# Attention decoder on one core: fp32 products for C, the inner norm's weight moved into a matrix, two norms moved to GpSimd, and a new hand-written order

## The chip, the cores and the metric

One core of a Trainium2 chip runs the whole program. The metric is the device time of one execution in microseconds (us), the median of three runs. The engines are called by their names in the trace: PE (TensorE, with PEld for its weight loads), DVE (VectorE), ACT (ScalarE), POOL (GpSimd), and SP (SyncE, which here only issues DMAs).

## The reference, cut to what matters

The input x is 128 sequences of 64 tokens by 128 features, ctx is as large. Everything is fp32.

```
def attn(x):                       # linear attention, 16 heads of 64, 32 features
    q, k, v = x @ Wq + bq, x @ Wk + bk, x @ Wv + bv
    qp, kp  = exp(q @ wq_feat), exp(k @ wk_feat)
    D_inv   = 1 / (qp . sum_n kp + 1e-6)
    context = einsum(kp, v)        # one 32 x 64 matrix a head
    return (qp @ context * D_inv) @ Wproj + bproj
def xattn(x, ctx):                 # softmax attention, 16 heads of 8
    return softmax(Q K^T / sqrt(8)) V @ Wo + bo
def ffn(x):
    h = gelu(x @ tern(W_fc).T)     # 128 -> 512, weights -1, 0 or 1
    h = (h - mean(h)) * rsqrt(var(h) + eps) * ln_w + ln_b
    return h @ tern(W_proj).T      # 512 -> 128
x = layernorm(x + attn(x)); x = layernorm(x + xattn(x, ctx)); x = layernorm(x + ffn(x))
```

## The kernel before, in words

The 128 sequences are 16 batches of 8. In every tile the 128 partitions hold features or tokens and the 512 columns are the 8 times 64 tokens. A batch goes through three blocks.

The first block: `k0` to `k3` and `q0` to `q3` are projections with exp behind them (three fp16 products each, of the two fp16 parts of x and of the weights). `ks`, `kst`, `dT` and `bc` make and spread the denominators. `g0` to `g7` (L329) form G = x^T kp, one sequence each, on 64 of the 128 rows of the array: the even ones on the upper half, the odd ones on the lower. An fp32 matmul shows as two instructions in the trace. `c0` to `c7` (L341) multiply each G by Mh, the product of Wv and Wproj of each head, which gives C; `o` multiplies qT by C. The 16 heads of a C take a column tile of 32 each, so that four run at once. Here G is kept as two fp16 parts, Gh (ACT, L581) and Gl (DVE, L822), and M as Mh and Ml: three fp16 products a head, 48 matmuls a C.

The second block: `x1s` (ACT L601, POOL L1081) splits x1 into fp16 parts, a transposing DMA turns it, `qproj`, `kproj`, `vproj` project, `qpack`, `kpack` and `rows` are DMAs that lay out rows for `score` and `prob`, `score` is followed by eight maxima on DVE (L880), `prob` by exp on ACT, `pv`, `oturn`, `cs` and `proj` end it.

The third block: `up0` to `up3` with GELU (ACT L675), `stat` (DVE, POOL), `gs` (POOL L1114), a multiplication of the 128x512 GELU output by ln_w, `gh` (ACT L688) and `gl` (POOL L1119), the fp16 parts, a transposing DMA, and `down0` to `down3`, eight fp16 products each (L507, L508), with `tpj`, the ternary weights.

The norms behind the blocks are `ap1` (ACT L595, with a shift that POOL works out in L1072 and L1076), `ap2` (ACT) and `ap3` (DVE L858); their inverse roots come from POOL (L1058, L1061). For the last two batches the transposes are done by PE, with other weights.

Order: three strings (HEAD, PERIOD, TAIL) list the steps. `g3@1` is step g3 of the batch one behind the period's own, a + puts the step's copy on ACT, not on DVE. PERIOD is run for n = 1 to 14. All engines go through one list, each does its own steps in that order and never passes a waiting one. The eight PSUM banks are dealt out in turn in the same order: a step's first matmul waits until the bank's last user, eight uses back, has been read.

Of the kernel before, what the change touches and what calls it, by code (L numbers as in the profile page):

```python
# [39 lines left out]
prob0@2 prob1@2 st1@1 st3@5 down0@4 ap1+@1 csplit@1 down1@4 ab2@3 ks pv0@2 kst g0+ x1s@1 g1+ g2+ g3 ab1@1 pv1@2 xb down2@4 split@-1 kproj@1 loadx@-1  # L40
q0 down3@4 q1 up0@3 c0 gs0@3 c1 up1@3 up2@3 stat@3 up3@3 qproj@1 oturn0@2 q2 loadc kpack@1 q3 c2+ oturn1@2 gs1@3 g4 g5 g6 g7 cs0@2 c3+ dT qpack@1
k0@-1 gl0@3 gh0@3 k1@-1 c4+ c5+ score0@1 k2@-1 cs1@2 proj0@2 score1@1 k3@-1 gh1@3 gs2@3 vproj@1 gl1@3 proj1@2 c6+ gs3@3 c7+ gh2@3 rows@1 gh3@3 st2@2
bc gl2@3 gl3@3 ap3@5 o ap2+@2
# [4 lines left out]
vproj@2 c0+@1 c1+@1 g4+@1 q0@1 q1@1 c2+@1 ap3@6 c3+@1 gl1@4 q2@1 st3@5 gh1@4 ap2+@3 gs3@4 kst@1 gl2@4 score0@2 q3@1 score1@2 gh2@4 g5@1 g6+@1 gl3@4
dT@1 kpack@1 c4@1 g7+@1 c5@1 gh3@4 kproj@1 down0@4 vproj@1 tw@1 c6+@1 c7@1 down1@4 bc@1 rows@2 ab1@2 up0@3 down2@4 ab2@3 up1@3 up2@3 down3@4 gs0@3
stat@3 up3@3 o@1 prob0@2 st1@1 gl0@3 ap3@5 gs1@3 gl1@3 prob1@2 qpack@1 st3@4 gs2@3 gh0@3 pv0@2 oturn0@2 pv1@2 oturn1@2 gs3@3 ap1+@1 flip+@1 proj0@2  # L50
gh1@3 qproj@1 proj1@2 ap2+@2 st2@2 down0@3 ap3@4 down1@3 ab2@2 flip3@2 gh2@3 gh3@3 score0@1 score1@1 up0@2 gl2@3 up1@2 up2@2 gl3@3 up3@2 rows@1
# [27 lines left out]
def decoder_kernel(nc, a, out):  # L79
# [3 lines left out]
    GS = 2.0 ** -4  # L83
    two = range(2)

    with ExitStack() as ctx:
# [451 lines left out]
        def act_program(e):  # L538
# [151 lines left out]
            for name, s, t, on_act in PLAN:  # L690
# [22 lines left out]
                elif name in ("k", "q", "g", "prob", "up", "gh"):  # L713
                    {"k": kexp, "q": qexp, "g": gmat, "prob": prob, "up": up, "gh": ghi}[name](s, t)
# [4 lines left out]
                elif on_act:  # L719
                    {"c": cmat, "turn": turn}[name](s, t)  # L720

        def dve_program(e):
# [16 lines left out]
            def mh(c2):  # L739
                for c in range(2 * c2, 2 * c2 + 2):  # L740
                    hi, lo_ = [v[:, :].rearrange("p (c k a n) -> p c k a n", c=2, k=4, a=2)[:, c // 2, :, c % 2, :] for v in (Mh, Ml)]
                    w.wait_ge(s_mhh, c + 1)
                    e.scalar_tensor_tensor(lo_, bank[uses["mh", 0, c][0]][:, :].rearrange("p (k n) -> p k n", k=4), 1 / GS, hi,
                                           ALU.mult, ALU.subtract).then_inc(emptied("mh", 0, c)[0], 1)

# [623 lines left out]
```

## Time and profile before

| | |
|---|---|
| median of 3 runs | 671.31 us (670.25 to 672.45) |
| profiled execution, its own time | 668.43 us |
| span of its instructions | 666.6 us |
| mean granted TensorE clock | 0.975 |
| PE, DVE, ACT, POOL busy | 589.2, 548.2, 489.1, 457.0 us |

The span runs from the first to the last instruction. An engine's busy time is the time in which at least one of its instructions was open, so that PE's holds also the latency behind the last matmul of a row. The times below are starts from the beginning of the span.

### The profile page before, as it was taken

To read this page: it belongs to the slowest core of one execution; us is meant where nothing else is said; L and a number is where in the kernel's file an instruction comes from. 1 tells how busy PE (TensorE), PEld (TensorE's weight loads), DVE (VectorE), ACT (ScalarE), POOL (GpSimd) and SP (SyncE) were. 2 spreads that over 40 slices of the span, in tenths; PEclk is the share of its full clock that TensorE was granted. 3 is DMA by queue.
4 is the path that set the end of the run, shared out by engine and by line. 5 is a ranking of instruction groups with operands and counts; after the bars stand their busy time and mean duration, and the time that the engine had idled before them with its cause. 6 is when DMAs were issued, how large, how long until landed. Compare 5 with 4: busy or idle time off the path is not lost.

```text
span 666.6 us, 35171 instructions
## 1 busy us (share of the span) xinstructions
PE 589.2 (88%) x15392; PEld 417.9 (63%) x15392; DVE 548.2 (82%) x1365; ACT 489.1 (73%) x922; POOL 457.0 (69%) x563
## 2 busy tenths in 40 slices
PE   8997898989899889989998899989899899897675
PEld 5774656576666657566666657566576657565363
DVE  1864677888878978998999898998899989888786
ACT  3655485969688786968798687968788787777543
POOL 3152143877777786886978778876888777976632
PEclk8998999999999999999999899999999999799689
DMA  8005040435534346534573347334354446352501
GB/s 331 33 2 137 5 136 16 120 76 120 82 76 131 83 137 93 126 76 122 92 117 103 84 137 94 119 81 131 84 93 128 83 137 100 97 97 48 131 3 47
DMA packets 116170, 65.14 MB, mean 98 GB/s; under 512 B 94321, under 2 KB 100850, under 8 KB 115890
## 3 DMA queue, kind: packets, MB, share of 16 engines
q1 hardware_dynamic: 116018, 62.91, 40.7%
q8 instruction: 121, 1.98, 1.2%
q14 instruction: 31, 0.25, 0.2%
HBM read 17.27 MB, written 4.19 MB: 32 GB/s over the span
## 4 chain that ended last, share of the span: by engine, by line
PE 31%; DVE 25%; DMA 10%; ACT 9%; SPq 8%; POOL 8%; issue 8%; POOLq 0%; DVEq 0%; ACTq 0%
SPq L1214 7%; DMA pack<-Ql 6%; DVE mx L880 5%; DVE st L845 5%; DVE yo L858 3%; DVE Ql L864 3%; PE bank L329 3%; PE bank L361 3%; PE bank L453 3%; DVE qT L818 2%; ACT L675 2%; DMA gT<-gs 2%; PE bank L341 2%; POOL rstd L1061 2%; PE bank L297 2%
## 5 line engine op out<-in xcount | busy, mean ns | idle before, releaser
L822 DVE SCALAR_TENSOR_TENSOR Gl<-bank,Gh 128x512 f16<-128x512 f32 x128 | 81.2, 684 | 18.9 <-ACT Gh L581 18.4
L341 PE MATMUL bank<-Mh,Gh 128*32 128x128 f16 x2048 | 94.8, 223 | 1.4 <-DVE Gl L822 0.7
L880 DVE TENSOR_REDUCE mx<-bank 128x8 f32<-128x512 f32 x128 | 79.1, 682 | 20.4 <-PE bank L418 20.4
L341 PE MATMUL bank<-Ml,Gh 128*32 128x128 f16 x2048 | 94.3, 221 | 1.1 <-issue 1.0
L341 PE MATMUL bank<-Mh,Gl 128*32 128x128 f16 x2048 | 94.3, 221 | 0.8 <-issue 0.6
L651 ACT ACTIVATE PT<-bank 128x512 f32<-128x512 f32 x128 | 65.0, 615 | 21.5 <-PE bank L439 21.4
L341 PEld LDWEIGHTS bank<-Mh,Gh 128*32 128x32 f16 x2048 | 55.6, 97 | 35.8 <-issue 19.8
L566 ACT ACTIVATE kp<-bank 128x512 f32<-128x512 f32 x64 | 39.8, 622 | 50.1 <-PE bank L280 49.9
L581 ACT ACTIVATE Gh<-bank 128x512 f16<-128x512 f32 x128 | 69.2, 619 | 8.8 <-PE bank L329 6.4
L1114 POOL TENSOR_TENSOR gall<-gall,lnr 128x512 f32<-128x512 f32 x56 | 71.7, 1280 | 3.9 <-DVE st L845 3.9
L1119 POOL TENSOR_TENSOR gs<-gall,gs 128x512 f16<-128x512 f32 x56 | 64.8, 1163 | 11.3 <-ACT gs L688 9.9
L329 PE MATMUL bank<-kp,xs 64*128 64x512 f32 x256 | 70.4, 620 | 0.0
L1061 POOL TENSOR_TENSOR rstd<-ve,mhalf 128x4 f32<-128x4 f32 x64 | 65.4, 1022 | 5.3
L595 ACT ACTIVATE x<-x,nmr,rstd 128x128 f32<-128x128 f32 x128 | 52.8, 494 | 17.4 <-POOL nmr L1076 17.2
L361 PE MATMUL bank<-Cb,qT 128*64 128x128 f32 x1024 | 59.4, 274 | 2.4 <-DVE qT L818 2.3
L545 ACT ACTIVATE Cb<-bank 128x512 f32<-128x512 f32 x95 | 55.6, 624 | 5.2 <-PE bank L341 4.4
L361 PEld LDWEIGHTS bank<-Cb,qT 128*64 128x64 f32 x1024 | 55.6, 137 | 5.2 <-DVE qT L818 4.8
L341 PEld LDWEIGHTS bank<-Ml,Gh 128*32 128x32 f16 x2048 | 56.5, 98 | 2.0 <-issue 2.0
L341 PEld LDWEIGHTS bank<-Mh,Gl 128*32 128x32 f16 x2048 | 56.1, 98 | 1.5 <-issue 1.5
L688 ACT ACTIVATE gs<-gall 128x512 f16<-128x512 f32 x56 | 36.0, 644 | 26.3 <-DMA gT<-gs 26.3
L573 ACT ACTIVATE qT<-bank,qb 128x512 f32<-128x512 f32 x64 | 42.4, 694 | 5.3 <-PE bank L288 4.9
L818 DVE TENSOR_TENSOR qT<-qT,bank 128x512 f32<-128x512 f32 x64 | 39.7, 682 | 7.8 <-PE bank L320 7.2
(194 smaller groups left out, 1661.3 us busy)
## 6 DMA issues: line engine op xcount, KB each, us to landing
pack<-Qh SPq DMA_DIRECT2D x64, 128.0 KB, 2.6
xT<-in_xT SPq DMA_DIRECT2D x16, 256.0 KB, 3.1
xs<-in_x_nat SPq DMA_DIRECT2D x16, 256.0 KB, 3.7
cxT<-in_cxT SPq DMA_DIRECT2D x16, 256.0 KB, 4.1
Kp<-Kh SPq DMA_DIRECT2D x32, 128.0 KB, 3.2
pack<-Ql SPq DMA_DIRECT2D x32, 128.0 KB, 2.7
out_y<-yo SPq DMA_DIRECT2D x15, 256.0 KB, 2.4
Kp<-Kl SPq DMA_DIRECT2D x16, 128.0 KB, 3.1
```

Of the source, the lines that this page charges most:

```text
L329: e.matmul(bk[:, :], xs[s % 2][r0:r0 + 64, tile(t)], kp[r0:r0 + 64, tile(t, 512)], start=True, stop=True).then_inc(done, 1)
L341: m = e.matmul(bk[32 * j:32 * j + 32, tile(g_)], G[b % 4][:, tile(hh, 32)], M[:, tile(hh)], start=(G is Gh and M is Mh), stop=(M is Ml))
L361: m = e.matmul(bk[64 * bb:64 * bb + 64, 0:128], qT[:, tile(8 * g_ + b, 64)], Cb[b][:, tile(g_)], start=False, stop=(g_ == 3))
L545: e.activation(dst, src, ACT.Copy, scale=scale).then_inc(emptied(name, s, t)[0], 1)
L581: e.activation(Gh[b % 4][:, :], bank[uses["g", s, b][0]][:, :], ACT.Copy, scale=GS).then_inc(s_gth, 1)
L651: e.activation(PT[tp][:, tile(j, 512)], bank[uses["prob", s, i][0]][:, :], ACT.Exp, scale=SM).then_inc(emptied("prob", s, i)[0], 1)
L818: e.tensor_tensor(v, v, bank[uses["bc", s, t][0]][:, :].rearrange(by_head, g=4), ALU.mult).then_inc(emptied("bc", s, t)[0], 1)
L822: e.scalar_tensor_tensor(Gl[b % 4][:, :], bank[uses["g", s, b][0]][:, :], GS, Gh[b % 4][:, :], ALU.mult, ALU.subtract).then_inc(emptied("g ...
L880: e.tensor_reduce(to, bank[uses["score", s, i][0]][:, :].rearrange("p (g b k) -> p g b k", g=2, b=4), AX.X, ALU.max).then_inc(emptied("sco ...
L1061: e.tensor_tensor(rstd[k][:, :], ve[k][:, :], mhalf[:, :], ALU.pow).then_inc(s_rstd[k], 1)
L1114: e.tensor_tensor(g[t][:, :], g[t][:, :], lnr[:, :], ALU.mult).then_inc(s_gs, 1)
L1119: e.tensor_tensor(gs[t % 2][:, 512:1024], g[t][:, :], gs[t % 2][:, 0:512], ALU.subtract).then_inc(s_gl, 1)
```

## The change

- C: G and M stay fp32 in one tile each (GT, Mh). A C is 16 fp32 matmuls instead of 48 fp16 ones; its stationary operand is 32 columns of GT, its moving operand 128 columns of Mh. Each G is copied once, by ACT or by DVE (four of the eight in PERIOD by each), instead of by ACT and then DVE.
- The inner norm's weight: ln_w is multiplied into the down projection's weights once, at the start, and the product is kept in two fp16 parts, tph and tpl. `down` has 12 products instead of 8; `gs` and the load of lnr go.
- `ap1` and `ap3` are done by POOL, as four tensor_scalar of 128x128 each; POOL's two small steps for ap1's shift go. `ap2` stays on ACT.
- HEAD, PERIOD and TAIL are new.

```
-wk wb small1 k0 WkT k1 k2 loadx zeros k3 mh0 mh1 g0+ g1+ split split@1 Wvp g2+ g3+ ...
+zeros mh0 mh1 wk wq k0 Wvp k1 WqT k2 q0 small1 wb nbeta WkT loadx g0+ g1+ g2+ Wff g3+ ...
...
-                for g_ in range(4):
-                    for G, M in ((Gh, Mh), (Gl, Mh), (Gh, Ml)):
-                        for j in range(4):
-                            hh = 4 * g_ + j
-                            m = e.matmul(bk[32 * j:32 * j + 32, tile(g_)], G[b % 4][:, tile(hh, 32)], M[:, tile(hh)], ...
+                for hh in range(H):
+                    g_, j = hh // 4, hh % 4
+                    m = e.matmul(bk[32 * j:32 * j + 32, tile(g_)], GT[b % 4][:, tile(hh, 32)], Mh[:, tile(hh)], start=True, stop=True)
...
                     for c in range(4):
-                        e.matmul(bk[:, 0:128], gT[t][:, tile(c)], tpj[:, tile(c)], start=(c == 0), stop=False)
-                        m = e.matmul(bk[:, 0:128], gT[t][:, tile(4 + c)], tpj[:, tile(c)], start=False, stop=(c == 3))
+                        e.matmul(bk[:, 0:128], gT[t][:, tile(c)], tph[:, tile(c)], start=(c == 0), stop=False)
+                        e.matmul(bk[:, 0:128], gT[t][:, tile(c)], tpl[:, tile(c)], start=False, stop=False)
+                        m = e.matmul(bk[:, 0:128], gT[t][:, tile(4 + c)], tph[:, tile(c)], start=False, stop=(c == 3))
...
-                w.wait_ge(*filled("g", s, b))
-                e.activation(Gh[b % 4][:, :], bank[uses["g", s, b][0]][:, :], ACT.Copy, scale=GS).then_inc(s_gth, 1)
+                copy("g", s, b, GT[b % 4][:, :])
...
-                w.wait_ge(s_gth, 8 * s + b + 1)
-                e.scalar_tensor_tensor(Gl[b % 4][:, :], bank[uses["g", s, b][0]][:, :], GS, Gh[b % 4][:, :],
-                                       ALU.mult, ALU.subtract).then_inc(emptied("g", s, b)[0], 1)
+                w.wait_ge(*filled("g", s, b))
+                e.tensor_copy(GT[b % 4][:, :], bank[uses["g", s, b][0]][:, :]).then_inc(emptied("g", s, b)[0], 1)
...
+            def apply(k, s, x):
+                w.wait_ge(s_rstd[k], s + 1)
+                for t in range(4):
+                    e.tensor_scalar(x[:, tile(t)], x[:, tile(t)], mv[k][:, 2 * t:2 * t + 1], rstd[k][:, t:t + 1], ALU.subtract, ALU.mult)...
...
-            def gscale(s, t):
-                w.wait_ge(s_Wff, 32)
-                w.wait_ge(s_st["4"], 4 * s + t + 1)
-                e.tensor_tensor(g[t][:, :], g[t][:, :], lnr[:, :], ALU.mult).then_inc(s_gs, 1)
```

What the new order does is seen in the engines' own sequences. PE in the middle of the program, around the O products (L361) of a batch, before (L320 spreads the denominators, L439 are the shifted scores for exp, L507 and L508 are down):

```order
L426 MATMUL bank<-small,mx 64x128
L320 MATMUL bank<-Dblk,small 128x128 x16
L352 MATMUL bank<-nbeta,Dblk 128x128 x4
L361 MATMUL bank<-Cb,qT 64x128 x32
L439 MATMUL bank<-pack,Kp 64x128 x64
L507 MATMUL bank<-tpj,gT 128x128
L508 MATMUL bank<-tpj,gT 128x128
```

and some rows on, between the two halves of the PV products (L453, L297 are the K sums, L375 the K projection of the second block):

```order
L297 MATMUL bank<-kp,small 32x128 x16
L453 MATMUL bank<-PT,Vblk 32x64 x32
L329 MATMUL bank<-kp,xs 128x512 x4
L453 MATMUL bank<-PT,Vblk 32x64 x32
L375 MATMUL bank<-cxs,xWh 128x512
```

PE at the same place in the changed kernel (L357 is O, L414 the scores, L327 is G, L295 the K sums, L337 is C):

```order
L318 MATMUL bank<-Dblk,small 128x128 x16
L276 MATMUL bank<-Wkfh,xh 128x512
L277 MATMUL bank<-Wkfl,xh 128x512
L278 MATMUL bank<-Wkfh,xl 128x512
L348 MATMUL bank<-nbeta,Dblk 128x128 x4
L357 MATMUL bank<-Cb,qT 64x128 x32
L414 MATMUL bank<-Kp,pack 128x64 x64
L327 MATMUL bank<-kp,xs 128x512 x3
L295 MATMUL bank<-kp,small 32x128 x16
L337 MATMUL bank<-Mh,GT 32x128 x16
```

The scores come right behind O, one K projection stands between the spreading of the denominators and O, and the first G of a batch run as three in a row instead of four. The other five G come as three (ahead of c1 to c3) and as two (between the halves of PV).

The start of PE's program, changed kernel (L236 is M, L206 the fill matmuls that write nothing of use, L216 the weights' folding):

```order
L236 MATMUL bank<-pack 128x128 x16
L206 MATMUL bank<-PT 128x256 x25
L216 MATMUL bank<-small,pack 128x64 x16
L276 MATMUL bank<-Wkfh,xh 128x512
```

and before:

```order
L208 MATMUL bank<-PT 128x256 x25
L218 MATMUL bank<-small,pack 128x64 x8
L226 MATMUL bank<-small 64x4
L227 MATMUL bank<-small 64x4
L278 MATMUL bank<-Wkfh,xh 128x512
```

The M products moved ahead of the fill, and both foldings behind it.

POOL in the same period of the changed kernel, from the split of x on (L1078 is ap3, then ap1):

```order
L1055 TENSOR_SCALAR ve<-mv 128x4
L1058 TENSOR_TENSOR rstd<-ve,mhalf 128x4
L1078 TENSOR_SCALAR yo<-yo,mv,rstd 128x128 x4
L1078 TENSOR_SCALAR x<-x,mv,rstd 128x128 x4
L1035 TENSOR_TENSOR x<-x,bias 128x512
L1035 TENSOR_TENSOR xb<-xs,biasA 128x512
L1083 TENSOR_TENSOR x1s<-x,x1s 128x512
L1115 TENSOR_TENSOR gs<-gall,gs 128x512 x2
```

Both norms now stand on POOL ahead of the split of x1 (L1083) and of two parts of the GELU output (L1115).

## Rows read from the trace of the kernel before

**Rows 1.** Page, busy us, share of the span, instructions of each engine

```profile
PE 589.2 (88%) x15392; PEld 417.9 (63%) x15392; DVE 548.2 (82%) x1365; ACT 489.1 (73%) x922; POOL 457.0 (69%) x563
```

**Rows 2.** Timeline, PE: start us, us, what; O products (first instructions of batches)

```profile
38.90 1.31 PE L361 MATMUL bank<-Cb,qT 128*64 128x128 f32 x20
...
144.95 3.28 PE L361 MATMUL bank<-Cb,qT 128*64 128x128 f32 x56
...
557.31 2.95 PE L361 MATMUL bank<-Cb,qT 128*64 128x128 f32 x50 [0.21 <-DVE qT L818]
604.50 3.71 PE L361 MATMUL bank<-Cb,qT 128*64 128x128 f32 x64
```

**Rows 3.** Busy us by stretch: length, PE, PEld, DVE, ACT, POOL, clock, DMA

```profile
142.70:555.10 412.40, 374.89 (x10462) 266.42 (x10462) 363.85 (x901) 331.24 (x628) 325.76 (x395) 1.00 0.48 104
555.10:608.20 53.10, 49.24 (x1104) 34.15 (x1107) 44.64 (x122) 38.40 (x69) 41.42 (x52) 0.94 0.45 97
```

**Rows 4.** Timeline, PE: two C, the K sums, a C, one G alone

```profile
20.21 0.24 PE L341 MATMUL bank<-Mh,Gh 128*32 128x128 f16 x4
...
21.57 1.05 PE L297 MATMUL bank<-kp,small 128*32 128x128 f32 x32
22.44 0.23 PE L341 MATMUL bank<-Mh,Gh 128*32 128x128 f16 x4
...
23.21 1.12 PE L329 MATMUL bank<-kp,xs 64*128 64x512 f32 x2
24.27 0.24 PE L341 MATMUL bank<-Mh,Gh 128*32 128x128 f16 x4
```

**Rows 5.** Timeline, PE, batch period at 301: down, four G, one 512-column product

```profile
301.37 0.23 PE L507 MATMUL bank<-tpj,gT 128*128 128x128 f16 x1
...
302.22 0.22 PE L508 MATMUL bank<-tpj,gT 128*128 128x128 f16 x1
...
304.27 1.99 PE L329 MATMUL bank<-kp,xs 64*128 64x512 f32 x8
306.19 1.10 PE L453 MATMUL bank<-PT,Vblk 128*32 128x64 f32 x64
307.68 0.38 PE L375 MATMUL bank<-cxs,xWh 128*128 128x512 f16 x1
307.89 0.38 PE L376 MATMUL bank<-cxs,xWh 128*128 128x512 f16 x1
```

**Rows 6.** Groups by line: engine, operation, tiles, count, busy us, mean ns, idle before

```profile
L822 DVE SCALAR_TENSOR_TENSOR Gl<-bank,Gh 128x512 f16<-128x512 f32 x128 | 81.2, 684 | 18.9 <-ACT Gh L581 18.4
L880 DVE TENSOR_REDUCE mx<-bank 128x8 f32<-128x512 f32 x128 | 79.1, 682 | 20.4 <-PE bank L418 20.4
L858 DVE TENSOR_SCALAR yo<-yo,mv,rstd 128x128 f32<-128x128 f32 x64 | 35.3, 613 | 1.6 <-POOL rstd L1061 1.6
```

**Rows 7.** The same view, POOL

```profile
L1114 POOL TENSOR_TENSOR gall<-gall,lnr 128x512 f32<-128x512 f32 x56 | 71.7, 1280 | 3.9 <-DVE st L845 3.9
L1024 POOL CAST xh<-xT 128x512 f16<-128x512 f32 x16 | 9.8, 611 | 41.9 <-DMA xT<-in_xT 41.9
L1058 POOL TENSOR_SCALAR ve<-mv 128x4 f32<-128x4 f32 x64 | 13.1, 204 | 20.2 <-DVE mv L852 15.6
L1053 POOL TENSOR_TENSOR Dblk<-Dv,small 128x128 f32<-128x128 f32 x16 | 6.4, 401 | 18.4 <-DVE Dv L810 18.4
```

**Rows 8.** Waits: who waited for whom, us in total, times, longest

```profile
PE bank L418 <- DMA pack<-Ql: 20.3, 14, 2.8
```

**Rows 9.** Timeline, PE, start of the program: fill, first folding

```profile
1.04 3.38 PE L208 MATMUL bank<-PT 128*128 128x256 f16 x15 [1.04 <-DVE mhalf L727]
6.10 1.90 PE L218 MATMUL bank<-small,pack 128*128 128x64 f32 x16
```

**Rows 10.** DMA issues: KB each, median us from issue to landing

```profile
pack<-in_Wvp SPq DMA_DIRECT2D x1, 1024.0 KB, 7.3
x2T<-x2s SPq DMA_TRANSPOSE x14, 4.6
```

More of the change, by code:

```diff
@@ L39 @@
 PERIOD = """
[L40 to L43, printed above, removed]
+cs1@3 c6+@1 loadx@-1 c7+@1 dT@1 kproj@1 down0@4 proj0@3 kpack@1 k0 proj1@3 st2@3 k1 k2 gl2@4 bc@1 gl3@4 k3 gh3@4 o@1 ab1@2 score0@2 score1@2 ap2+@3
@@ L44 @@
+g0+ split@-1 g1+ g2+ st1@1 ks c0+ down1@4 q0 ap3@5 down2@4 ap1@1 up0@3 up1@3 ab2@3 down3@4 xb rows@2 up2@3 up3@3 gh0@3 x1s@1 g3 g4 gl0@3 gl1@3 qpack@1
+gh1@3 g5 c1 st3@4 c2 c3 prob0@2 csplit vproj@1 stat@3 q1 q2 prob1@2 pv0@2 oturn0@2 g6+ loadc@-1 cs0@2 kst gh2@3 g7 c4+ c5+ pv1@2 oturn1@2 q3 qproj@1
 """
 TAIL = """
-loadc@1 st3@6 prob0@3 st1@2 g0+@1 csplit@2 prob1@3 ks@1 down0@5 ap1+@2 ab2@4 x1s@2 cs0@3 down1@5 pv0@3 kpack@2 oturn0@3 pv1@3 xb@1 qpack@2 down2@5
-gs0@4 oturn1@3 up0@4 up1@4 down3@5 up2@4 cs1@3 gs1@4 stat@4 up3@4 gs2@4 gl0@4 g1+@1 kproj@2 g2@1 qproj@2 g3@1 gh0@4 proj0@3 proj1@3 st2@3 csplit@1
@@ L48 @@
[L48 to L51, printed above, removed]
@@ L52 @@
-turn0@2 ab1@1 down2@3 down3@3 st3@3 stat@2 prob0@1 prob1@1 turn1+@2 pv0@1 oturn0@1 pv1@1 oturn1@1 proj0@1 turn2+@2 proj1@1 st2@1 down0@2 turn3@2
-down1@2 ap3@3 ap2+@1 down2@2 ab2@1 down3@2 flip3@1 st3@2 up0@1 up1@1 up2@1 up3@1 turn0+@1 stat@1 ap3@2 turn1+@1 turn2+@1 down0@1 down1@1 down2@1
-turn3+@1 down3@1 st3@1 ap3@1
+kpack@2 k0@1 ab1@3 proj0@4 c6+@2 c7@2 cs1@4 dT@2 gl2@5 k1@1 proj1@4 st2@4 kproj@2 vproj@2 bc@2 ap2+@4 k2@1 o@2 st1@2 gh3@5 g0+@1 ap3@6 gl3@5 ab2@4
+g1@1 k3@1 score0@3 score1@3 down0@5 up0@4 ks@1 gh0@4 ap1@2 up1@4 up2@4 kst@1 up3@4 down1@5 rows@3 x1s@2 gl0@4 gl1@4 c0+@1 ab1@2 down2@5 down3@5 gh1@4
@@ new lines @@
+stat@4 prob0@3 c1@1 qpack@2 prob1@3 g2@1 g3@1 pv0@3 oturn0@3 qproj@2 pv1@3 g4+@1 csplit@1 oturn1@3 cs0@3 g5+@1 gh2@4 gl2@4 cs1@3 c2@1 c3+@1 down0@4
+down1@4 gh3@4 q0@1 kpack@1 q1@1 proj0@3 gl3@4 proj1@3 st2@3 kproj@1 q2@1 q3@1 xb@1 score0@2 ap2+@3 dT@1 g6+@1 g7+@1 score1@2 c4+@1 c5+@1 st3@5 c6+@1
+bc@1 ab2@3 rows@2 down2@4 up0@3 ap3@5 up1@3 gl0@3 down3@4 up2@3 up3@3 stat@3 gh0@3 gh1@3 c7@1 o@1 st1@1 ap1@1 prob0@2 prob1@2 ab1@1 st3@4 gh2@3 pv0@2
+oturn0@2 flip+@1 pv1@2 oturn1@2 gl1@3 qproj@1 proj0@2 proj1@2 st2@2 down0@3 vproj@1 ap2+@2 down1@3 qpack@1 flip3@2 score0@1 gh3@3 gl2@3 tw@1 up0@2
@@ L55 @@
+gl3@3 up1@2 score1@1 up2@2 down2@3 up3@2 rows@1 ap3@4 ab2@2 turn0@2 down3@3 prob0@1 prob1@1 stat@2 pv0@1 turn1+@2 oturn0@1 pv1@1 turn2+@2 oturn1@1
+proj0@1 ap2+@1 down0@2 proj1@1 st2@1 down1@2 st3@3 ap3@3 ab2@1 turn3@2 down2@2 down3@2 flip3@1 up0@1 up1@1 up2@1 st3@2 up3@1 ap3@2 turn0+@1 turn1+@1
+stat@1 down0@1 turn2+@1 down1@1 turn3+@1 down2@1 down3@1 st3@1 ap3@1
 """
@@ L153, in decoder_kernel @@
         ms = x2s[:, :].bitcast(F32)
-        gs, gTs, lnr = [sb(f"gs{i}", 1024, F16) for i in two], sb("gT", 4096, F16), sb("lnr", 512)
+        gs, gTs, tph, tpl = [sb(f"gs{i}", 1024, F16) for i in two], sb("gT", 4096, F16), sb("tph", 512, F16), sb("tpl", 512, F16)
         gT = [gTs[:, 1024 * t:1024 * t + 1024] for t in range(4)]
@@ L553, in mh @@
                     o = Mh[:, :].rearrange("p (c k a n) -> p c k a n", c=2, k=4, a=2)[:, c // 2, :, c % 2, :]
-                    w.wait_ge(*filled("mh", 0, c))
-                    e.activation(o, bank[uses["mh", 0, c][0]][:, :].rearrange("p (k n) -> p k n", k=4), ACT.Copy, scale=1 / GS).then_inc(s_mhh, 1)
+                    copy("mh", 0, c, o, shape="p (k n) -> p k n")
             def nbeta_():
@@ L737, in xw @@
                 e.tensor_tensor(xWl[:, :], xWall, xWh[:, :], ALU.subtract).then_inc(s_xwl, 1)
[L739 to L744, printed above, removed]
             def sel_():
@@ L848, in stats @@
                     w.wait_ge(s_rstd[k], s)
+                if s > 0 and k != "4":
+                    w.wait_ge(s_ln[k], 4 * s)
                 if s > 0 and k == "4":
@@ L973, in dve_program @@
                     pv(s, t)
-                elif not on_act and name in ("c", "turn"):
-                    {"c": cmat, "turn": turn}[name](s, t)
+                elif not on_act and name in ("g", "c", "turn"):
+                    {"g": gmat, "c": cmat, "turn": turn}[name](s, t)
                 elif name == "qproj":
@@ L982, in dve_program @@
                     stats(name[2], s, [x[s % 2][:, tile(i)] for i in range(4)], ready)
-                elif not on_act and name in ("ap1", "ap2", "ap3"):
+                elif not on_act and name in ("ap2",):
                     apply(name[2], s, {"ap1": x1, "ap2": x2, "ap3": yo}[name][s % 2])
@@ L1149, in pool_program @@
             for name, s, t, on_act in PLAN:
+                if name in ("ap1", "ap3"):
+                    apply(name[2], s, {"ap1": x1, "ap2": x2, "ap3": yo}[name][s % 2])
                 if name == "zeros":
```

56 lines of the change are left out of this document (30 added, 26 removed).

## The prediction

> **What bounds the kernel now.** I first read the page's busy shares [rows 1]: PE 88%, DVE 82%, ACT 73%, POOL 69%. That is an average, so I cut the span. The first instructions of O mark the batches [rows 2]: from the fourth batch to the fifteenth O starts 11 times later, 144.95 to 557.31, which is 37.5 us a batch with every step running. In that stretch [rows 3] PE is busy 374.9 of 412.4 us (34.1 a batch), DVE 363.9 (33.1), ACT 331.2 (30.1), POOL 325.8 (29.6). So no engine is full; PE and DVE are close, and each waits for the other through the banks. The last batch's O comes 47.2 us after its forerunner's [rows 2], and from its start to the end of the span 62.1 us pass, a chain through all engines.
>
> Busy holds latency tails, so I also laid PE's work end to end by the distance between starts. A product of 512 columns takes 0.215 us (307.68 to 307.89) [rows 5], 38 of them a batch: 8.2. A 128-column fp16 product, or four in column tiles, takes 0.057: the down's 16 starts span 0.85 [rows 5], and two C (24 groups of four) 1.36 (20.21 to 21.57) [rows 4]; 152 of them a batch: 8.6. Eight G take 2 x 1.92 = 3.8 [rows 5]. With O (3.7 and 0.4 of preparation), PV, scores and the rest about 32.5 us. So PE idles or sits in handovers about 5 us of each 37.5. The waits view names no single culprit: its longest entry for PE is the scores' wait for the packed Q, 20.3 us in all [rows 8].
>
> **The change on PE, a batch.** C: the K sums (L297) have exactly the new shape, 128x128 fp32 in column tiles of 32, 16 matmuls, 32 instructions in the trace. They take 0.87 (21.57 to 22.44) [rows 4] where a C now takes 0.68, so +0.2 each, 8 a batch: +1.6. Both ends of this price are near: 0.85 by 32 instructions at that rate without handover, 0.89 at most.
> Down: 12 products instead of 8, at 0.057, four times: +0.9, for 14 of the 16 batches.
> G: four in a row, two couples on different halves of the array, take 1.92, so 0.96 a couple; a G alone takes 1.06 (23.21 to 24.27) [rows 4, 5]. Rows of three, three and two are two couples with a single behind each and one couple: 3 x 0.96 + 2 x 1.06 = 5.0 instead of 3.8. Since the lone one may overlap its neighbours a little I take +1.0, between 0 and +1.2.
> Sum +3.5: PE's work laid end to end goes from 32.5 to 36.0 of a period that is now 37.5.
>
> **The others, a batch.** DVE loses the eight Gl (81.2/16 = 5.1) [rows 6], gains four G copies and one C copy at 0.68 (+3.4), and loses the third norm (2.2): 33.1 to 29.2. ACT loses four G copies, one C copy and ap1 and gains nothing. POOL loses `gs`, 71.7/14 = 5.1 [rows 7], and 0.4 of shift, and gains eight tensor_scalar of 128x128. No such row exists. From below: 0.20, the same instruction with 4 columns; from above: 0.61, a cast of 512 columns. The nearest is 0.40, two inputs of 128x128; this one reads one, so I take 0.35 and 2.8 a batch: 26.9. All three are covered by PE's 36.0. Here is a rule against the change: the Trainium skill (GPSIMD Engine Reference, Key points) calls the vector engine structurally about twice as fast for elementwise work. By it, VectorE's 0.55 [rows 6] would be 1.1 here, 8.8 a batch instead of 2.8; the sum goes by 2.8, the rule is a rival below.
>
> **What waits are left.** So PE becomes the bound, and the question is how much of its 5 us of gaps stays. I placed one period on PE's new sequence, with the rows' durations on the others. Four places are tight. (1) The scores now come right ahead of G, and the eight maxima on DVE, 0.6 us apart (682 ns each, overlapped) [rows 6], free the banks of the three G, the K sums and C: about 0.3 us of wait. (2) up0 needs x2 transposed: ap2, split on POOL, then 4.6 us to landing [rows 10]; it lands within half a microsecond of its use: 0 to 1. (3) The second PV waits for the second row of exps on ACT: 0.3. (4) Packed Q has 2.6 us of room, where before it had none; that wait should go. With the handovers this makes 0.9 us of gap and 36.9 us a batch as the lower bound. The upper bound is that the 5 us stay: 41.0. A PE that full has no slack for a late DMA, and the layout by hand lets none be late; so I take a gap of 2.3, nearer the lower bound since DVE, ACT and POOL all got lighter: 38.3 a batch. Over 11 batches: (38.3 - 37.5) x 11 = +8.8.
>
> **Start and end.** The fill (25 matmuls, 1.04 to 6.10, 0.2 us each) ran while the first weights travelled [rows 9]. Now M comes first; it waits for 1 MB (7.3 us as third load [rows 10], less as the first) and the fill and both foldings stand behind it. About 5 us of what was free lands on the path: +5 (0 to +7). The first three batches get +2.5 each for C and G: +7.5; their periods took 35.4 each (38.90 to 144.95) [rows 2] though most of the third block, up and down with 3.5 us of PE, was not there yet, so over 6 us of each were gaps, and I give back 3.3 each: -10. Between the last two O's POOL is busy 41.4 of 53.1 us [rows 3], a chain in which `gs` stands four times a batch; PE has 41 us of work there: -2. The last chain loses two POOL steps ahead of ap1: -1.
> Sum: 8.8 + 5 + 7.5 - 10 - 2 - 1 = +8.3. The profiled execution is 668.4 (span 666.6), so 676.7; the median of the runs shown is 671.3, so 679.6, say **680 us**.
>
> **The rivals.**
> - *The lighter engines give PE back its gaps* (faster). For it: DVE, ACT and POOL all drop by 3 to 4 us a batch, and the gaps came from their coupling. Against it: it asks for 97.5% of PE. It decides at 37.5 us a batch, a gap of 1.5. With the laid-out 36.9: 15.4 less than my sum, 664 us. Chance 0.28.
> - *Gain and loss meet*, 37.5 to 37.7 a batch: 670 to 673. The three G in a row costing no more than before would do it, -1.0 x 11 from the forecast gives 669. Chance 0.12.
> - *POOL's norms are dear.* At 1.1 us each, ap3 and ap1 take 8.8 instead of 2.8, and since ap1 stands behind ap3, x1's split, its transpose and the parts of the GELU output come 6 us later, at the end of their room: about 40 a batch, +1.7 x 11 = 19 more, 699. Chance 0.05.
> - *The change is not what its words say*: "G in pairs" is, by the sequence, 3, 3, 2. I have priced what the sequence shows.
>
> **How the numbers follow.** Forecast 0.55 for 38 to 39 a batch, with the dear norms 0.60 for slower; 0.28 faster; 0.12 within 0.3% (2 us, about what this measurement can tell from no change). The range goes down to the faster case with 2 us of start given back, 662, and up to a gap of 3.7, 15.4 more than the sum, 696. Slower's own range is 674 to 696.
>
> **What would show it.** In the changed profile C should be 0.87 a piece, PE busy 36 to 37 us a batch and over 93% between the fourth and fifteenth O; DVE below 80%. O's distance there is the test: below 37.3 my gap is wrong, above 39.5 something else is the bound. POOL's new rows show 0.35 or not. The first O's place shows the start. If PE's share falls while the time rises, I was wrong on the bound itself.

## The result and the profile after

The changed kernel takes **697.71 us** (median of 4 runs, 696.17 to 699.64), the kernel before 670.78 (665.73 to 672.45): ratio 1.0435, interval 1.0378 to 1.0491. Forecast were 680 us, range 662 to 696. The direction was right and the size was not: 18 us too low, and the measured time lies 2 us above the range. Ratios below leave out runs that lie well above a kernel's others: some of the kernel before, and the profiled one of b3_fold.

The first O of batches, the same view as [rows 2] (start, length, instructions), in the changed kernel, where O is L357:

```profile
53.73 2.51 PE L357 MATMUL bank<-Cb,qT 128*64 128x128 f32 x42
...
150.71 1.53 PE L357 MATMUL bank<-Cb,qT 128*64 128x128 f32 x24
...
579.82 3.71 PE L357 MATMUL bank<-Cb,qT 128*64 128x128 f32 x64
...
624.88 3.39 PE L357 MATMUL bank<-Cb,qT 128*64 128x128 f32 x58
```

These four starts and the span, 694.3, cut the miss into stretches. The forecast for each is the row of before plus the prediction's terms:

| stretch | before | forecast | after | miss |
|---|---|---|---|---|
| start to the fourth batch's O | 144.95 | 147.45 | 150.71 | +3.3 |
| 11 full periods | 412.36 (37.49 each) | 421.2 (38.3) | 429.11 (39.01) | +7.9 |
| fifteenth to sixteenth O | 47.2 | 45.2 | 45.1 | -0.1 |
| last O to the end | 62.1 | 61.1 | 69.4 | +8.3 |

So two places hold most of it: the periods and the last chain. The start hides two misses that cancel: the first O comes 14.8 us later than before (53.7 against 38.9), where +5 and a batch's +2.5 were forecast, and the three periods behind it take 32.3 us each instead of the 35.4 of before. By stretch, the view of [rows 3], with the last chain added (length, then PE, PEld, DVE, ACT, POOL, clock, DMA share, GB/s):

```profile
150.70:579.80 429.10, 414.06 (x9230) 297.41 (x9226) 324.28 (x838) 294.52 (x529) 334.37 (x416) 1.00 0.50 101
624.90:694.30 69.40, 44.72 (x721) 34.91 (x717) 41.81 (x135) 30.78 (x55) 43.53 (x59) 0.80 0.20 47
```

PE is busy 96.5% of the full periods, 37.6 us a batch, which looks like the forecast bound. The groups by line (busy us, mean ns | idle before) say what else is new:

```profile
L337 PE MATMUL bank<-Mh,GT 128*32 128x128 f32 x4096 | 126.4, 274 | 0.1
L881 DVE TENSOR_REDUCE mx<-bank 128x8 f32<-128x512 f32 x128 | 78.1, 680 | 0.9 <-PE bank L414 0.4
L1078 POOL TENSOR_SCALAR x<-x,mv,rstd 128x128 f32<-128x128 f32 x64 | 50.2, 802 | 0.5
L1078 POOL TENSOR_SCALAR yo<-yo,mv,rstd 128x128 f32<-128x128 f32 x64 | 50.2, 797 | 0.4
```

**A norm instruction on POOL takes 0.80 us.** The prediction took 0.35 with 0.61 as its upper bound. POOL's share is therefore 30.4 us a batch in full periods, not 26.9. DVE's maxima, which waited 20.4 us for the scores before [rows 6], wait 0.9. The waits view names who stands behind the new rows (us in total, times, longest; SPq is the DMA queue that SP feeds):

```profile
ACT x1s L597 <- POOL x L1078: 35.2, 14, 4.2
PE bank L435 <- ACT PT L647: 12.9, 11, 2.5
SPq L1256 <- POOL yo L1078: 112.6, 14, 19.9
```

The PE wait of [rows 8], for the packed Q, went as forecast. One period shows how 6.3 us of POOL reach PE. Timeline of POOL, then ACT, then PE (start, length, in brackets the idle time ahead and what ended it):

```profile
355.40 3.14 POOL L1078 TENSOR_SCALAR yo<-yo,mv,rstd 128x128 f32<-128x128 f32 x4
358.52 3.13 POOL L1078 TENSOR_SCALAR x<-x,mv,rstd 128x128 f32<-128x128 f32 x4
361.60 1.28 POOL L1035 TENSOR_TENSOR x<-x,bias 128x512 f32<-128x512 f32 x1
...
358.43 0.63 ACT L687 ACTIVATE gs<-gall 128x512 f16<-128x512 f32 x1
361.68 0.63 ACT L597 ACTIVATE x1s<-x 128x512 f16<-128x512 f32 x1 [2.62 <-POOL x L1078]
362.21 0.61 ACT L687 ACTIVATE gs<-gall 128x512 f16<-128x512 f32 x1
362.85 1.28 ACT L647 ACT_TABLE_LOAD   x1
364.14 2.06 ACT L647 ACTIVATE PT<-bank 128x512 f32<-128x512 f32 x4
...
362.08 0.64 PE L435 MATMUL bank<-pack,Kp 64*64 64x128 f16 x32
...
365.86 0.83 PE L435 MATMUL bank<-pack,Kp 64*64 64x128 f16 x32 [1.07 <-ACT PT L647]
```

ap3 stands ahead of ap1, so x1 is ready at 361.6. ACT's split of x1 waits 2.62 us for it with the exps behind it, and PE's second half of the shifted scores waits 1.07 us for the exps. Nothing in this chain is PE's. Waits of this kind sum to 12.9 us, where PE is idle 15.0 us in all in the eleven periods.

### The profile page after: what moved, and what is told of

It is laid out like the page before. It is cut to its first block, busy times and chain, and to the rows that moved or that the text cites. A ratio compares the mean times of both kernels' runs of the same rounds, so it can differ in the third digit from the quotient of the medians.

```text
span 694.3 us, 31347 instructions
## 1 busy us (share of the span) xinstructions
PE 637.0 (92%) x13568; PEld 460.2 (66%) x13568; DVE 491.7 (71%) x1246; ACT 437.9 (63%) x783; POOL 479.7 (69%) x603
## 4 chain that ended last, share of the span: by engine, by line
PE 56%; POOL 17%; DVE 14%; ACT 6%; issue 5%; DMA 1%; SPq 1%; POOLq 0%; DVEq 0%; ACTq 0%
PE bank L337 10%; PE bank L357 8%; DVE mx L881 7%; PE bank L327 6%; POOL yo L1078 6%; POOL x L1078 5%; PE bank L449 4%; POOL rstd L1058 3%; ACT PT L647 2%; PE bank L318 2%; PE bank L306 2%; ACT L647 2%; DVE st L844 2%; PE bank L435 2%; DVE qT L814 2%
## 5 line engine op out<-in xcount | busy, mean ns | idle before, releaser
L337 PEld LDWEIGHTS bank<-Mh,GT 128*32 128x32 f32 x4096 | 109.8, 110 | 30.0 <-issue 19.5
L337 PE MATMUL bank<-Mh,GT 128*32 128x128 f32 x4096 | 126.4, 274 | 0.1
L327 PE MATMUL bank<-kp,xs 64*128 64x512 f32 x256 | 91.8, 633 | 0.0
L543 ACT ACTIVATE GT<-bank 128x512 f32<-128x512 f32 x67 | 39.7, 605 | 61.9 <-PE bank L327 61.9
L647 ACT ACTIVATE PT<-bank 128x512 f32<-128x512 f32 x128 | 65.7, 610 | 5.0 <-PE bank L435 4.9
L822 DVE COPY GT<-bank 128x512 f32<-128x512 f32 x61 | 40.6, 686 | 39.5 <-PE bank L327 25.4
L1115 POOL TENSOR_TENSOR gs<-gall,gs 128x512 f16<-128x512 f32 x56 | 64.4, 1173 | 1.4 <-ACT gs L687 1.4
L1055 POOL TENSOR_SCALAR ve<-mv 128x4 f32<-128x4 f32 x64 | 12.5, 196 | 68.5 <-DVE mv L853 64.6
L357 PE MATMUL bank<-Cb,qT 128*64 128x128 f32 x1024 | 59.4, 274 | 0.0
L357 PEld LDWEIGHTS bank<-Cb,qT 128*64 128x64 f32 x1024 | 55.6, 137 | 1.9
L327 PEld LDWEIGHTS bank<-kp,xs 64*128 64x128 f32 x256 | 32.3, 185 | 29.5 <-issue 14.5
L1078 POOL TENSOR_SCALAR x<-x,mv,rstd 128x128 f32<-128x128 f32 x64 | 50.2, 802 | 0.5
L1078 POOL TENSOR_SCALAR yo<-yo,mv,rstd 128x128 f32<-128x128 f32 x64 | 50.2, 797 | 0.4
L814 DVE TENSOR_TENSOR qT<-qT,bank 128x512 f32<-128x512 f32 x64 | 39.7, 681 | 12.9 <-PE bank L318 12.7
L786 DVE STREAM_TRANSPOSE OT<-bank 128x512 f32<-128x512 f32 x32 | 22.9, 717 | 36.3 <-PE bank L449 36.2
L504 PE MATMUL bank<-tph,gT 128*128 128x128 f16 x224 | 40.5, 220 | 1.3 <-DMA gT<-gs 1.3
L1035 POOL TENSOR_TENSOR x<-x,bias 128x512 f32<-128x512 f32 x32 | 41.0, 1282 | 0.7 <-PE bank L364 0.7
```

The lines of the kernel that those rows point to most:

```text
L327: e.matmul(bk[:, :], xs[s % 2][r0:r0 + 64, tile(t)], kp[r0:r0 + 64, tile(t, 512)], start=True, stop=True).then_inc(done, 1)
L337: m = e.matmul(bk[32 * j:32 * j + 32, tile(g_)], GT[b % 4][:, tile(hh, 32)], Mh[:, tile(hh)], start=True, stop=True)
L357: m = e.matmul(bk[64 * bb:64 * bb + 64, 0:128], qT[:, tile(8 * g_ + b, 64)], Cb[b][:, tile(g_)], start=False, stop=(g_ == 3))
L543: e.activation(dst, src, ACT.Copy, scale=scale).then_inc(emptied(name, s, t)[0], 1)
L647: e.activation(PT[tp][:, tile(j, 512)], bank[uses["prob", s, i][0]][:, :], ACT.Exp, scale=SM).then_inc(emptied("prob", s, i)[0], 1)
L814: e.tensor_tensor(v, v, bank[uses["bc", s, t][0]][:, :].rearrange(by_head, g=4), ALU.mult).then_inc(emptied("bc", s, t)[0], 1)
```

## The experiments

Three rounds each, on the same chip as runs of the kernel before. O0 is the first O, "period" the mean over the 11 full ones, "end" the last O to the end of the span. These three come from one profiled execution of each kernel. An a-kernel starts from the changed kernel, a b-kernel from the one before.

| kernel | median us | ratio, interval | O0 | period | end |
|---|---|---|---|---|---|
| before | 670.78 | 1 | 38.9 | 37.49 | 62.1 |
| after | 697.71 | 1.0435, 1.0378 to 1.0491 | 53.7 | 39.01 | 69.4 |
| a1_ap3_dve | 678.36 | 1.0149, 1.0100 to 1.0198 | 53.9 | 37.41 | 70.0 |
| a3_both_dve | 676.45 | 1.0117, 1.0069 to 1.0165 | 53.8 | 37.56 | 65.7 |
| b1_pool | 750.62 | 1.1232, 1.1167 to 1.1297 | 39.3 | 42.46 | 78.6 |
| a8_swap | 713.88 | 1.0673, 1.0600 to 1.0745 | 54.0 | 40.42 | 68.7 |
| b2_c32 | 663.77 | 0.9924, 0.9885 to 0.9964 | 40.3 | 37.50 | 61.8 |
| b3_fold | 682.35 | 1.0149, 1.0064 to 1.0234 | 40.7 | 38.59 | 63.1 |
| b4_c32_fold | 674.06 | 1.0063, 1.0026 to 1.0100 | 38.6 | 38.39 | 62.2 |
| a4_two | 691.23 | 1.0317, 1.0266 to 1.0367 | 53.2 | 38.60 | 69.1 |
| a10_both_dve_two | 673.53 | 1.0081, 1.0041 to 1.0120 | 54.4 | 37.19 | 68.5 |
| a5_fill | 694.22 | 1.0369, 1.0306 to 1.0432 | 49.7 | 39.07 | 67.5 |
| a9_act_fill | 702.61 | 1.0508, 1.0446 to 1.0571 | 53.5 | 39.01 | 73.4 |
| b5_g3_act | 663.68 | 0.9942, 0.9901 to 0.9982 | 40.9 | 37.43 | 61.7 |

### One norm, then both, back on VectorE: a1_ap3_dve, a3_both_dve

```
# a1: ap3's four tensor_scalar are issued by DVE; a3: ap1's as well
-                elif not on_act and name in ("ap2",):
+                elif not on_act and name in ("ap2", "ap3"):      # a3: ("ap1", "ap2", "ap3")
...
-                if name in ("ap1", "ap3"):
+                if name in ("ap1",):                             # a3: neither
```

> The changed kernel with the third norm back on DVE, ap1 still on POOL. Theory N (the norms on POOL cost most of what I missed: 0.80 us each instead of 0.35, ap3 ahead of ap1 on POOL): ap1 comes 3.1 us earlier in each batch, ACT's wait for it goes, and the three ap3 near the end leave the last chain; 697.7 down by 12 to 20, about 680. Theory P (PE full at 37 us a batch whatever POOL does): only the last chain gains, 4 to 6, about 692.

> The changed kernel with both norms on DVE (ap1 takes about 2.2 us of DVE more a batch than ACT's did here). N: about 676, O to O 37.5 to 38 us instead of 39.0, and 62 us from the last O to the end instead of 69. P: O to O stays 39.0, only the last 69 us shrink to 62: about 690.

Measured: 19.4 us less with one norm moved, 21.3 with both, as theory N said. Its words on the end did not hold: the last chain is 70.0 us in a1, not shorter, and 65.7 in a3, not 62. The full periods by stretch, a1, then a3:

```profile
151.20:562.70 411.50, 408.19 (x9230) 295.57 (x9226) 334.53 (x878) 293.33 (x529) 307.04 (x376) 1.00 0.50 104
```

```profile
151.40:564.50 413.10, 410.56 (x9230) 294.84 (x9226) 367.55 (x922) 294.52 (x529) 266.42 (x332) 1.00 0.48 104
```

In both PE is busy over 99% of the stretch, 37.1 and 37.3 us a batch: now it is PE that bounds. Of the 1.6 us by which a1's period is shorter, 1.1 are idle time of PE and 0.5 are busy time for the same number of products; where that half microsecond comes from is not shown. What made the period 39.0 was the queue of two norms on POOL; with ap3 gone from it, ap1 may stay there at no cost to the period, since ACT waits 5.4 us in all for it instead of 35.2. SP, too, waits less for ap3, 84.1 us instead of 112.6:

```profile
ACT x1s L597 <- POOL x L1078: 5.4, 3, 4.2
...
SPq L1256 <- DVE yo L859: 84.1, 14, 16.0
```

The same eight instructions cost DVE very unequal times. The stretch around ap3 in a3 (DVE, then POOL), then in a1:

```profile
350.43 3.04 DVE L859 TENSOR_SCALAR yo<-yo,mv,rstd 128x128 f32<-128x128 f32 x4
353.66 1.10 DVE L859 TENSOR_SCALAR x<-x,mv,rstd 128x128 f32<-128x128 f32 x4
...
350.64 1.27 POOL L1035 TENSOR_TENSOR x<-x,bias 128x512 f32<-128x512 f32 x1
351.87 1.27 POOL L1035 TENSOR_TENSOR xb<-xs,biasA 128x512 f32<-128x512 f32 x1
```

```profile
349.19 1.08 DVE L859 TENSOR_SCALAR yo<-yo,mv,rstd 128x128 f32<-128x128 f32 x4
...
349.53 3.33 POOL L1078 TENSOR_SCALAR x<-x,mv,rstd 128x128 f32<-128x128 f32 x4
```

Four in 1.1 us while POOL idles or runs its tensor_scalar, four in 3.04 while POOL adds two tensors: DVE finishes 0.3 us after POOL's second addition ends. So DVE's own price is 0.28 each. The 0.55 of [rows 6] is a mix of the same kind: in the kernel before, four take 1.11 us at 558.96, with POOL idle for most of it, and more beside a row of POOL's subtractions and a cast:

```profile
296.22 3.64 DVE L858 TENSOR_SCALAR yo<-yo,mv,rstd 128x128 f32<-128x128 f32 x4
```

The Trainium skill (SBUF — State Buffer, "SBUF: two separate sides") describes this as an exclusive lock on a port pair that the two engines share; a3's rows agree with it. The overlap in a1 does not show it: there DVE runs at its own price and only POOL pays, 3.33 us for its four instead of 3.13.

### The norms alone, in the old order: b1_pool

```
# kernel before, with ap1 and ap3 as POOL's apply(), and gh1@3 of the tail one place up
+            def apply(k, s, x):
+                w.wait_ge(s_rstd[k], s + 1)
+                for t in range(4):
+                    e.tensor_scalar(x[:, tile(t)], x[:, tile(t)], mv[k][:, 2 * t:2 * t + 1], rstd[k][:, t:t + 1], ...
```

> The kernel before with ap1 and ap3 on POOL and nothing else (one gh of the tail moved up so that no engine waits in a circle). POOL then carries 29.6 + 6.2 us a batch. N: slower by 15 or more, 685 to 700. P: the norms are hidden but for the end, 675 to 680.

Measured: 12.3% slower, 750.6 us, far above both forecasts. The period grows by 5.0 us for 6.3 us of norms put on POOL, the last two O's lie 8.5 us further apart, and the end is 16.5 us longer. Part of this goes with PE's granted clock, which is 0.95 in the periods where it was 1.00 before; PE's busy time is 1.7 us a batch more at the same work. Waits in b1:

```profile
ACT x1s L600 <- POOL x L1084: 56.3, 15, 7.9
PE bank L374 <- POOL cxs L1038: 47.4, 14, 5.1
```

The old order has POOL's split of ctx right behind ap1, and PE's K projection waits for it 14 times. In the new order the same move costs 1.5 us a period (39.0 against a3's 37.6). So the new order bears the norms on POOL better, and still they cost more than they give.

### ap1 ahead of ap3: a8_swap

```
-g0+ split@-1 g1+ g2+ st1@1 ks c0+ down1@4 q0 ap3@5 down2@4 ap1@1 up0@3 up1@3 ...
+g0+ split@-1 g1+ g2+ st1@1 ks c0+ down1@4 q0 ap1@1 down2@4 ap3@5 up0@3 up1@3 ...
```

> The changed kernel with ap1 ahead of ap3 in the repeated part of the order, so that POOL does ap1 first; no engine's work changes, the head and the tail stay. If the harm between the O's is ap1's lateness (ACT's x1s waits for it with the exps behind): ap1 comes 3.1 us earlier, O to O goes from 39.0 to 37.5, 11 to 13 times, 678 to 684. If it is POOL's load: no change, 697.

Neither forecast held: the wait that looked like the culprit shrank, and the kernel became 16 us slower. Waits in a8:

```profile
ACT x1s L597 <- POOL x L1078: 9.1, 4, 4.2
PE bank L435 <- DMA pack<-Mrow: 23.0, 11, 2.3
SPq L1256 <- POOL yo L1078: 143.5, 14, 19.5
```

On SP the store of y (L1256) stands ahead of the DMA that lays out the maxima's rows (L1229). SP waits for ap3 112.6 us in all in the changed kernel and 143.5 here; the rows come late, and PE waits for them where before it waited for exps. So either order of two 3.1 us norms makes something late: x1 for ACT, or y for SP. This is read from the waits; a kernel with the store of y behind the rows' DMA was not run.

### Parts of the change on the kernel before: b2_c32, b3_fold, b4_c32_fold

b2 has only fp32 C, in the old order; b3 only ln_w in the down weights; b4 both. Both norms stay on ACT and DVE.

```
# b2
-                    for G, M in ((Gh, Mh), (Gl, Mh), (Gh, Ml)):
...
+                for hh in range(H):
+                    g_, j = hh // 4, hh % 4
+                    m = e.matmul(bk[32 * j:32 * j + 32, tile(g_)], GT[b % 4][:, tile(hh, 32)], Mh[:, tile(hh)], start=True, stop=True)
# b3: gs dropped from the order, tph and tpl made at the start
+                        e.matmul(bk[:, 0:128], gT[t][:, tile(c)], tpl[:, tile(c)], start=False, stop=False)
```

> The kernel before with C as fp32 products and one copy of each G, old order. PE gets 0.2 x 128 = 25 us more work, DVE 38 us less. P: PE's work counts in full, +15 to +25, 686 to 696. N: the gaps take up most of it because DVE gets lighter, -5 to +10, 666 to 681.

> The kernel before with only the inner norm's weight folded: gs gone from POOL (72 us), down with 12 products (+12 us of PE), old order. If PE's work counts in full: +12, about 682. If the gaps take it up, as they did for C, and POOL's relief counts: -3 to -8, about 664.

> The kernel before with fp32 C and the folded weight, old order, norms on ACT and DVE: beside the changed kernel with both norms on DVE (676.5) it differs in the order alone. If the new order is good, this is slower, 680 or more; if the new order costs (start +5 to +10, three G in a row +1 a batch, longer end), this is 658 to 668.

Full periods by stretch, b2, then b4:

```profile
143.00:555.50 412.50, 390.04 (x9054) 279.72 (x9054) 344.44 (x865) 312.39 (x572) 325.01 (x395) 1.00 0.45 104
```

```profile
142.50:564.80 422.30, 400.09 (x9229) 289.78 (x9229) 350.06 (x865) 313.29 (x572) 271.70 (x351) 1.00 0.44 101
```

Against [rows 3] b2 has 15.2 us more PE work in the stretch (1.4 a batch; forecast 1.6) and the same period, 37.50: PE's gaps shrank from 3.4 to 2.0 us a batch and took it, while DVE has 1.8 us a batch less. The whole kernel is 0.8% *faster*; by its trace the gain lies outside the full periods (fourth O at 143.0 instead of 144.95, last two O 45.1 apart instead of 47.2). b4 adds 0.9 us of PE a batch, exactly the forecast price of the down's four extra products, and now the period grows by the same 0.9 (37.50 to 38.39). POOL's 4.8 us a batch less bought nothing. PE's gap is 2.0 us a batch in both. The first addition was free and the second cost its full price. b3, the folded weight alone, agrees: its ratio of 1.0149 is 10 us (the median 682.35 still holds the profiled run, without it 679.7), near the 10.3 between the medians of b2 and b4, with an interval from 4 to 16 us. b4 itself, 674.1, lies between its two forecasts.

From b4 to a3 only the order differs, and ap1, which is on ACT there and on DVE here. PE's busy time rises by 1.0 a batch (the forecast price of G in 3, 3, 2), its gap falls from 2.0 to 0.2, and the period falls by 0.8. The start (fourth O 8.9 us later) and the end (3.5 us longer) take more than that back. In all a3 is 2.4 us slower than b4 by medians, which is hardly clear of noise: the intervals of the two ratios overlap.

### Less work on PE: a4_two, a10_both_dve_two

```
# four of the twelve down products go, from the changed kernel (a4) and from a3 (a10)
-                        e.matmul(bk[:, 0:128], gT[t][:, tile(c)], tpl[:, tile(c)], start=False, stop=False)
```

> The changed kernel without the product with tpl (the down projection leaves out the small part of its weights), norms still on POOL: 12.5 us of PE less. If PE bounds each batch: 685. If POOL's norms, through ACT and the exps, set the pace: 693 to 697, and PE waits longer for the exps instead.

> Both norms on DVE and the product with tpl left out (the down projection leaves out the small part of its weights). With the norms out of the way PE is the bound: all of the 12.5 us come back, 664. If DVE (81% busy here) bounds it instead: 670 to 675.

0.9 us a batch of PE work taken out gives 0.41 a period in a4 and 0.37 in a10. So a4, 691.2, lies between its two forecasts, and a10, 673.5, meets the second of its own. The full periods of a10:

```profile
150.98:560.08 409.10, 400.01 (x9059) 284.68 (x9055) 367.39 (x922) 294.32 (x529) 266.64 (x333) 1.00 0.50 105
```

PE's gap has grown from 0.2 to 0.8. So even with cheap norms PE is the bound only just; behind it stands something near 37.2 us. DVE is busy 90% of these periods, ACT 72% and POOL 65%, so DVE is the likeliest, but no run here separates it from ACT or the handovers.

### The fill at the start: a5_fill, a9_act_fill

```
-FILL = {("wk", 0, 0): 25, ("rows", 15, 0): 2}
+FILL = {("mh", 0, 0): 25, ("rows", 15, 0): 2}
# a9 also: ap1 on ACT with its shift, as before, and ap3 on DVE
```

> The changed kernel with the 25 fill matmuls ahead of the M products, in the time in which the first weights travel. My price for the start says 3 to 5 us come back: the first O at 49 to 51 us instead of 53.7 and 693 to 695. If the start is set by the loads and not by PE: no change, 697.

> The changed kernel with ap1 on ACT as before, ap3 on DVE as before, and the fill ahead of the M products. Against 676.5 with both on DVE: the fill gives 3, ACT's norm saves DVE 2 us a batch: 670 to 674. If ACT's wait for POOL's shift blocks the GELUs behind it: 680 or more.

PE's first rows in the changed kernel, then in a5:

```profile
5.76 3.79 PE L236 MATMUL bank<-pack 64*128 64x128 f32 x32 [5.76 <-DMA pack<-in_Wvp]
9.48 3.51 PE L206 MATMUL bank<-PT 128*128 128x256 f16 x25
12.82 3.68 PE L216 MATMUL bank<-small,pack 128*128 128x64 f32 x32
```

```profile
1.04 5.51 PE L206 MATMUL bank<-PT 128*128 128x256 f16 x25 [1.04 <-DVE mhalf L726]
6.49 2.18 PE L236 MATMUL bank<-pack 64*128 64x128 f32 x32
8.60 3.79 PE L216 MATMUL bank<-small,pack 128*128 128x64 f32 x32
```

The folding starts 4.2 us earlier, the first O 4.0, the fourth 4.6 (146.1), and the median falls by 3.5: the part of the forecast +5 that stood for the fill was right in place and near in size. Of the 4.2 us, 1.6 are the M products themselves, which take 2.18 instead of 3.79 when the fill has run ahead of them.

a9 got none of it in its first O. PE paused 0.88 us for a weight matrix, until 8.66, and two to three microseconds later its granted clock fell: 1.00 up to 11.0, 0.51 from 11 to 18. By stretch (clock is the third number from the end):

```profile
5.70:13.30 7.60, 6.69 (x65) 6.53 (x66) 0.69 (x1) 2.66 (x5) 1.77 (x2) 0.86 1.03 412
13.30:18.00 4.70, 4.70 (x13) 1.65 (x13) 0.69 (x1) 2.39 (x4) 1.26 (x2) 0.51 0.71 269
```

That is the 1.2 GHz level; the projections came 0.43 us apart instead of 0.215. a5, without the pause, kept 1.00 throughout; that the pause was the cause is read from this one pair. The time, 702.6, is a9's second forecast. Its period is 39.01, as with both norms on POOL. ACT waits 32.5 us in all for POOL's shift, the GELUs queue behind ap1, and they hold the banks of the next products:

```profile
PEld bank L327 <- ACT gall L674: 21.4, 11, 2.0
```

The new order leaves ACT no room for ap1 at that place; DVE and POOL have it.

### A version that beats both: b2_c32, and b5_g3_act

```
-prob0@2 ... ks pv0@2 kst g0+ x1s@1 g1+ g2+ g3 ab1@1 ...
+prob0@2 ... ks pv0@2 kst g0+ x1s@1 g1+ g2+ g3+ ab1@1 ...     # on b2: g3's copy on ACT
```

> The kernel before with fp32 C, and one more G copy on ACT instead of DVE. If DVE still sets the pace in the old order: 2 to 5 us below 663.8. If PE does: the same within 2 us.

663.68 us, not to be told from b2's 663.77: by its forecast this speaks against DVE as what sets the pace there. The best kernel here is the old one with fp32 C and nothing else of the change, 0.8% below before (interval 0.4 to 1.2%): small, but seen in 10 runs of each of the two.

## Why the prediction was wrong in size

The parts, taken in the order in which the runs stack them, by medians that come from different chips: fp32 C -7.0 (b2), ln_w in the weights +10.3 (b2 to b4), the new order +2.4 (b4 to a3), the norms on POOL +21.3 (a3 to after). The ratios, each against runs of before on the kernel's own chip, give -5, +9, +4 and +21. The parts do not simply add: in the old order the norms alone cost 80. The prediction went wrong in the last.

- **"So I take 0.35 and 2.8 a batch: 26.9."** This is the step that failed. The term measured 0.80 and 6.3 a batch, above the upper bound of 0.61. The two bounds were the wrong rows: a cast of 512 columns does not bound four calls with per-partition scalars from above, and 0.20 for 4 columns only bounds it from below. The row called the nearest, 0.40 for two inputs of 128x128, is half of what this instruction with one input takes. Between 4 and 128 columns the same instruction grows by 0.6 us, 4.8 ns a column, where the 512-column cast [rows 7] takes 1.2 ns a column in all. The rule that was weighed there (the Trainium skill, GPSIMD Engine Reference, Key points) gave the estimate of 1.1. The measured 0.80 lies between; against DVE's undisturbed 0.28 the ratio is 2.9, not 2.
- **"All three are covered by PE's 36.0."** It followed from the price. At 0.80 the block of two norms is 6.3 us on POOL, and what counts is not POOL's total (30.4 of 39.0, still covered) but the block's place: x1 late for ACT, or y late for SP. The rival "POOL's norms are dear" named this mechanism and ended at 699 us, 1 from the result, with a chance of 0.05. Its parts were less right: it put the norms at 1.1 and the period at 40, and gave the end nothing. So its closeness to the result is partly luck.
- **"PE becomes the bound."** True at 37.4 us (a1, a3), not at 39.0. PE laid end to end was 36.0 in the forecast; busy time carries 1.6 more than the laid-out 32.5 in [rows 3], so 36.0 would show as about 37.6; 37.1 to 37.3 were measured. The terms for down (+0.9; measured 0.9 from b2 to b4) and G (+1.0; measured 1.0 from b4 to a3) were right. C measured three in 2.76 us, 0.92 each, not 0.87.
- **"I take a gap of 2.3."** Without the dear norm the period is 37.4, 0.9 under the forecast 38.3: the new order closes gaps better than I trusted, 0.2 to 0.3 us left. Over the eleven periods that is 10 us. That a1 (678.4) lies near 680 is therefore luck: this error cancels the next one and the start's.
- **"The last chain: -1."** It is +7.3. Pricing it only by the two POOL steps that go was a second step that failed. From the last O to the last batch's shifted scores 30.3 us pass before (604.5 to 634.8), 29.3 and 30.9 in the two kernels with both norms on DVE (a3, a10), and 32.0 to 33.5 in the five of the new order with ap1 on POOL (after, a1, a4, a5, a8): about 2 to 3 us, of which POOL's 3.1 instead of DVE's 1.1 explain 2. From there to the end it is 31.4 to 31.9 in the old tail with the norms off POOL (before and b2 to b5), 34.6 in the old tail with them on it (b1), 36.9 after, and 35.2 to 37.6 in the six others that share its tail, on whatever engine the norms run: some 5 us that belong to the new tail. I had priced the tail's change at nothing. Part of it goes with PE's granted clock, which in this stretch is 0.92 before and 0.76 after; but at 0.90 (a5) the new tail still takes 3.4 us more than before. Which step of it costs them was not tried.
- **The start, +5, and "above 39.5 something else is the bound".** The fill's share stood (a5), the start as a whole did not: the first O came 14.8 us later, and the first periods gave back more than forecast. The test did not stand either: at 39.0 another bound was already there. PE's 96.5% busy could not show it, the 35.2 us wait of ACT for POOL did.

The chain of waits in the changed kernel's last 62 us shows POOL in DVE's place (start, length, what):

```profile
632.29 3.15 POOL x L1078 x4
...
673.82 2.34 POOL yo L1078 x3
...
678.90 0.74 POOL yo L1078
...
679.69 2.35 POOL yo L1078 x3
...
689.81 2.34 POOL yo L1078 x3
```

## What to carry to other kernels

Price a moved instruction by its own form on the new engine. Where no row has that form, run it alone first, or widen the range by the ratio of the engines, not by the nearest other instruction. Look at the block that it makes in its new queue and at who stands behind it, ACT and the DMA queue included: a queue that is busy 78% can still set the period. And split a change into its parts before judging it: here one part gains 0.8%, the order is about even, and the two others lose more.

## What the runs showed of the hardware

- POOL's tensor_scalar of 128x128 fp32 with two per-partition scalars: 0.80 us, with 128x4 0.20, while its tensor_tensor of two 128x128 fp32 inputs takes 0.40; at the very end, with DVE idle, still 3.13 for four.
- DVE's same instruction: 0.28 us by itself or beside POOL's tensor_scalar (whose four then take 3.33), 0.76 beside POOL's additions of two 128x512 tensors. Moving work off POOL can so make DVE's rows longer: ap3's rows sum to 17.5 us in a1 and 37.2 in a3.
- 16 fp32 matmuls in column tiles of 32 (128x128) take 0.92 us where 48 fp16 ones took 0.68, and yet b2, which does only this, is 0.8% faster. A G needs one copy there instead of two passes; that this is why was not tried by itself.
- A pause of 0.88 us in PE's first ten microseconds (a9, until 8.66) was followed by a granted clock at the 1.2 GHz level from about 11 to 18 us; the same start without the pause (a5) kept 2.4 GHz.
